# Re-dealing the first score pass of two attention stages over a longer share of each head group

## The reference, cut to what matters

```python
scores = jnp.einsum('bqhd,bkhd->bhqk', q, k) / np.sqrt(hd)
scores = jnp.where(causal, scores, finfo.min)      # the second layer: 0 <= q - k <= 127
attn = jax.nn.softmax(scores, axis=-1)
o = jnp.einsum('bhqk,bkhd->bqhd', attn, v)
```

## Time and profile before

| | |
|---|---|
| median of three runs | 1845.01 us (1844.8 to 1847.09) |
| the profiled execution's own time | 1847.77 us |
| its span, first to last instruction | 1846.0 us |
| PE busy | 1471.7 us, 80% |
| VectorE busy | 1132.5 us, 61% |
| ScalarE busy | 700.3 us, 38% |
| POOL busy | 288.7 us, 16% |
| mean granted PE clock | 0.879 |
| stage b, second passes | about 344 to 866 us of the span |
| stage d, second passes | about 1355 to 1724 us |

### The profile page before, as it was taken

How to read it: one execution, slowest core, us unless ns; L and a number is a source line. 1 busy time by engine, 2 the same in 40 slices (tenths; PEclk the granted TensorE clock), 3 DMA queues, 4 the chain that set the end, 5 groups by cost and what they waited for, 6 DMA issues and landing times. The chain is left out here.

```text
span 1846.0 us, 31979 instructions
## 1 busy us (share of the span) xinstructions
PE 1471.7 (80%) x10886; PEld 1161.7 (63%) x10886; DVE 1132.5 (61%) x2505; ACT 700.3 (38%) x1428; POOL 288.7 (16%) x224
## 2 busy tenths in 40 slices
PE   2578777988888978888398999788588978889565
PEld 1467676665555645555287888677476767677435
DVE  3676663775775676673455443566576766758486
ACT  1122231353444434445253553343223423234275
POOL 1111021203003003200000002751212220200000
PEclk9699797898988978989698999889798989899888
DMA  4000015216026117210542333320556252330001
GB/s 125 1 1 1 0 45 135 58 57 174 8 81 164 29 35 199 61 35 2 176 150 63 104 101 104 92 65 7 144 135 167 64 148 52 105 97 2 4 1 67
DMA packets 102314, 141.09 MB, mean 76 GB/s; under 512 B 30307, under 2 KB 91084, under 8 KB 102156
## 3 DMA queue, kind: packets, MB, share of 16 engines
q1 hardware_dynamic: 86034, 120.93, 22.8%
q0 software_dynamic: 12672, 13.45, 2.7%
q10 hardware_dynamic: 3456, 4.77, 0.9%
HBM read 77.17 MB, written 61.27 MB: 75 GB/s over the span
## 5 line engine op out<-in xcount | busy, mean ns | idle before, releaser
L1251 ACT ACTIVATE b_probs<-b_ps 125x500 f32<-125x500 f32 (+1 forms) x352 | 187.2, 568 | 153.7 <-PE b_ps L1114 137.5
L1501 DVE TENSOR_REDUCE b_neg<-b_ps 125x1 f32<-125x500 f32 (+3 forms) x304 | 183.6, 644 | 70.7 <-PE b_ps L1079 61.3
L1073 PE MATMUL b_ps<-b_k_st,b_q_st 96*125 96x500 bf16 (+3 forms) x512 | 153.2, 346 | 40.2 <-DVE b_neg L1501 16.3
L1251 ACT ACTIVATE d_probs<-d_ps 125x504 f32<-125x504 f32 (+1 forms) x176 | 100.4, 589 | 171.7 <-PE d_ps L1114 154.0
L1110 PE MATMUL b_ps<-b_q_st,b_k_st 99*125 99x500 bf16 (+3 forms) x512 | 147.5, 340 | 12.9 <-ACT b_probs L1251 10.6
L1501 DVE TENSOR_REDUCE d_neg<-d_ps 125x2 f32<-125x504 f32 (+2 forms) x176 | 114.9, 677 | 50.6 <-PE d_ps L1076 44.7
L1073 PEld LDWEIGHTS b_ps<-b_k_st,b_q_st 96*125 96x125 bf16 x512 | 75.2, 152 | 81.9 <-DVE b_neg L1501 29.5
L1073 PE MATMUL d_ps<-d_k_st,d_q_st 96*125 96x252 bf16 (+2 forms) x384 | 100.1, 294 | 24.8 <-DMA d_k_st<-scratch_stacks 15.3
L180 PE MATMUL c_ps<-c_hd,c_dw_hi 128*128 128x500 f32 x192 | 80.1, 417 | 45.5 <-DVE c_ag L2164 25.4
L1110 PE MATMUL d_ps<-d_q_st,d_k_st 99*125 99x252 bf16 (+2 forms) x384 | 94.1, 281 | 23.5 <-ACT d_probs L1251 13.8
L1110 PEld LDWEIGHTS b_ps<-b_q_st,b_k_st 99*125 99x125 bf16 x512 | 69.0, 147 | 56.4 <-ACT b_probs L1251 39.3
(11 more groups left out here) (381 smaller groups left out, 4012.9 us busy)
## 6 DMA issues: line engine op xcount, KB each, us to landing
scratch_stacks<-b_part SPq DMA_DIRECT2D x48, 375.0 KB, 4.6
scratch_stacks<-d_part SPq DMA_DIRECT2D x48, 375.0 KB, 4.6
b_q_st<-scratch_stacks SPq DMA_DIRECT2D x16, 562.5 KB, 5.4
b_k_st<-scratch_stacks SPq DMA_DIRECT2D x16, 562.5 KB, 7.0
d_q_st<-scratch_stacks SPq DMA_DIRECT2D x16, 562.5 KB, 5.1
d_k_st<-scratch_stacks SPq DMA_DIRECT2D x16, 562.5 KB, 6.6
c_xrows<-scratch_slots SPq DMA_DIRECT2D x54, 128.0 KB, 2.1
c_ew_raw<-in_L_ffn_ew_dram SPq DMA_DIRECT2D x24, 256.0 KB, 6.6
```

Of the source, the lines that this page charges most:

```text
L1073: mm = pe.matmul(out, q_st[0:STACK, hh, i * TT:(i + 1) * TT], k_st[0:STACK, hh, k0:k0 + n], start=True, stop=True)
L1251: act.activation(dst, second_out(x, unit), ACT.Exp).then_inc(c["exp"].sem, 1)
L1501: dve.tensor_reduce(dst, ps[:TT, bank, 0:per * n].rearrange("p (m n) -> p m n", n=n), AX_X, ALU.max, negate=True).then_inc(free_sem(t, p), 1)
```

## The change

Four numbers of each stage's plan: AHEAD stays, FIRSTS_BY goes from 0.60 to 0.80 (b) and from 0.673 to 0.90 (d), the turn goes from 0.783 to 0.90 and from 1.0 to 1.08, max_in from 0.943 to 1.0 and from 1.148 to 1.18. All are counted from t0 and in groups.

```diff
-    AHEAD, FIRSTS_BY, TURN_AT, MAX_IN_AT = (0.383, 0.673, 1.0, 1.148) if local else (0.219, 0.60, 0.783, 0.943)
+    AHEAD, FIRSTS_BY, TURN_AT, MAX_IN_AT = (0.383, 0.90, 1.08, 1.18) if local else (0.219, 0.80, 0.90, 1.0)
```

## The result

The changed kernel takes 1891.1 us (median of four runs) against 1844.9 before: 46 us more. The ratio is 1.0240, with a 95% interval of 1.0216 to 1.0264. The forecast was 1870 with a range up to 1886, so the direction was right, the size too small by almost half, and the time lies 5 us above the range.

The account below looks back on a forecast made before the run. PE was taken as the bound almost everywhere, so only its waits and granted clock could move. Stage d's plus 28 and stage b's minus 3.5 made about 25 us, from 1845.0 to 1870, range 1846 to 1886.

Parts of the forecast that it names:

- The hand-over to groups 2 and 3: Stage d: rows queue behind the next batch's load; 14.6 us at group 3, batches 1 and 2; 7.3 in batch 0.
- The 0.7 us at group 0: Stage d, hand-over to the next batch's group 0: rows meet the load of group 3; 0.7 us three times, 2.1.
- The first cut: Stage d, batches 1 and 2: turn's copies behind VectorE's cut free back~4's bank late; 1.2 us each, bounds 0 and 2.2.
- The turn's wait for the maxima in stage d: Stage d, turn of group 2: comes at about 1507.9, no wait of PE for the maxima counted.
- ScalarE's list: Stage d: exponentials behind the hand-over in ScalarE's order; no term, nothing counted.
- The last batch: Stage d, no load near: groups 2 and 3 come about 0.7 us later each; plus 1.5 us.
- Stage b: Sum of the terms for stage b: minus 3.5 us.
- The turn's new wait at the norm: Stage b, layer norm: turn2 needs maxima behind norm and three reductions; plus 1.0 us net, three times, bounds -2 and +2.5.
- The gain at F*0.0: Stage b, reload of the stacked keys: three F units fill the wait; minus 1.3 us, three times, bounds -3 and 0.
- The rows don't queue behind the load: Rival, stage d: the 24 us of collisions go, 0.7 us comes in four places; 1849 us, chance 0.14.
- Faster, since stage b is thinner: Rival: half of stage b's 15.8 us reduction waits and 7 us of lower clock go, collisions absent; 1834 us, chance 0.12.
- Worse: Rival: batch 0 collides in both places (+7), the wait at b's norm costs its upper bound (+7); 1884 us, chance 0.08.

Follow-up runs that it names:

- the single edits: Changed kernel with one stage d edit each: load waits for next group's first S unit, 1858.2 us; group 1's turn early, 1874.8; group 2's F units early, 1880.3.
- the three together: Changed kernel with all three of the single edits in stage d at once, stage b as changed: 1851.1 us, ratio 1.0052.

## Why the prediction was wrong in size

- **The hand-over to groups 2 and 3** was right in its mechanism. Place, order and spacing came out to a tenth of a microsecond, the total of the wait was 27.0 for "near 25", and the clock fell to the lower level behind each. Batch 0, counted at half, collided in both places (5.88 and 4.93); at the same time a wait of 4.92 for exponentials inside its group 2, behind a weight load, went away. The 0.7 us at group 0, three times, did not come: no S0.0 of batches 1 to 3 waits for its rows. The net price of the collisions, 29 undone in the changed kernel less 14 undone in the kernel before, is 15. The forecast had 24, so this term was, if anything, too large.
- **The first cut** is the term that was mis-sized. The forecast took 1.2 us in two batches, 2.4 in all, with 2.2 a batch as the upper bound. Its mechanism was right (VectorE "only then frees the bank that back~4 needs"). Measured are 8 us at the cuts, 2 to 4 in each, and 13 for the whole kernel when the turn is put back. PE's wait grew by 2.6 in batches 1 and 2, since a wait of 3.0 behind the same cut was there already. It grew by 1.9 in batch 0, which the forecast left out. The lower clock behind the cut, 0.50 to 0.57 for 4 us in the three batches (0.50 to 0.73 before), was not in the term either.
- **The turn's wait for the maxima in stage d** was put at nothing. The forecast let the turn of group 2 come "at about 1507.9", as if "final" would end 1.7 us sooner with that much VectorE work moved behind it, and gave PE no wait there. In the changed kernel "final" still waits 1.31 us for POOL, the last reduction and the maxima follow it until 1.84 us behind its end (1523.03 to 1524.87), and PE waits 2.1 to 2.3 us at this turn in all four batches: 10.8 us in stage d instead of 2.7. Late F units alone cost 16 us.
- **ScalarE's list** was put at nothing, too. The forecast followed VectorE's and SP's lists, and not the exponentials behind the hand-over: 7 us of waits (8.7 against 1.8). The last batch, forecast at plus 1.5, shows the last two costs without any load near: 5.3 us from its first S unit to the end of the stage (1698.3 to 1766.0, before 1661.4 to 1723.8).
- **Stage b** had the wrong sign, minus 3.5 for a measured plus 4. The waits for reductions at F units fell by 10, more than the 3.6 forecast, but the same reductions stand ahead of the transposes of the hd steps, plus 9.2, which the forecast had not looked at. The turn's new wait at the norm was forecast and came (2.2 to 3.0 us). The gain at F*0.0 was 1.4 us (15.2 to 13.8), not 3.9.
- **The rivals.** "The rows don't queue behind the load" (1849) is refuted by the two runs with the load behind the rows. "Faster, since stage b is thinner" saw a wait fall, and not where its work went. "Worse" (1884) was nearest in time, but by luck: half of its reason came, as batch 0 collided in both places, and the rest of the time came from the terms above.

The effects don't add: the single edits give 29, 13 and 7 (the last not clear of noise), and the three together 35 (1.0240 to 1.0052). So the steps that failed are named by the runs, but their shares of the 20 us that the forecast lacked are not settled one by one.

## What to carry to other kernels

When a step is placed later, list for every engine that takes part in it what stands right behind it in that engine's order, and price that too; here VectorE's cut (8 us), VectorE's maxima (8 us more of waits) and ScalarE's exponentials (7 us of waits) stood there, and the forecast had 4 for all of it. A wait that goes away on the critical engine has not gone until the work it waited for is found somewhere harmless: look at the next instructions that need the same engine. And a large prefetch that nobody needs for tens of microseconds should be made to wait until the small urgent transfer beside it has landed: one changed wait gave 14 us here.

## What was not expected of the hardware

Where a load and rows met, the packets of the two DMA queues moved in the order in which the transfers were issued. In the changed kernel, at the hand-over to group 3 in batch 1, the packets by queue (q10 has ScalarE's rows, 8 packets each; q1 SP's load, 112 packets a part) in the stretches 1548.0 to 1550.6, 1550.6 to 1552.7, 1552.7 to 1553.5, 1553.5 to 1555.2 and 1555.2 to 1556.2 us, with the share of 16 engines' time:

```profile
q10 hardware_dynamic: 8, 0.01, 0.8%
...
q1 hardware_dynamic: 92, 0.53, 90.3%
...
q1 hardware_dynamic: 46, 0.20, 97.8%
q10 hardware_dynamic: 8, 0.01, 3.3%
...
q1 hardware_dynamic: 65, 0.36, 91.1%
...
q10 hardware_dynamic: 8, 0.01, 2.5%
```

The first row passes at once. The second moves only with the last packets of the load's first part, some 2.5 us later, and the third with the last of the second part, another 2.5 us later, though all three rows were issued within 1.85 us. The hand-over to group 3 in batch 2 and the one to group 2 in batch 1 of the kernel before show the same three steps. Three rows of 5.9 KB thus take 6.9 us from the start of their issue, and 2.7 us with no load between them. The Trainium skill, page DMA: Bandwidth & Descriptors, section on queues, rings and completion order, has each engine take turns between the queues that have work; here, with whole transfers of 112 packets in between, no turns are seen. What makes the order is not shown.
